# Attention kernel: V product in plain f32, mask inside the row maximum, first rope on VectorE

## The reference, cut to what matters

```python
q = apply_rotary(x @ Wq_h, cos, sin)        # rope: t * cos + rotate_half(t) * sin
k = apply_rotary(x @ Wk_g, cos, sin)
scores = (q @ k.T) * 128 ** -0.5             # positions after the query are hidden
out += (softmax(scores) @ (x @ Wv_g)) @ (Wo_h * head_scale[h])
```

## Time and profile before

| | |
|---|---|
| median of 3 runs | 1413.64 us (1412.12 to 1413.68) |
| the profiled execution's own time | 1417.51 us |
| its span, first to last instruction | 1415.7 us |
| granted TensorE clock, mean | 0.97 of full speed |
| busy: PE / PE weight loads | 1265.8 us (89%) / 1118.0 us (79%) |
| busy: DVE / ACT / POOL | 823.7 (58%) / 734.8 (52%) / 687.0 us (49%) |

### The profile page before, as it was taken

How to read it: one execution, slowest core, us unless ns; L and a number is a source line. 1 busy time by engine, 2 the same in 40 slices (tenths; PEclk the granted TensorE clock), 3 DMA queues, 4 the chain that set the end, 5 groups by cost and what they waited for, 6 DMA issues and landing times. The chain is left out here.

```text
span 1415.7 us, 23253 instructions
## 1 busy us (share of the span) xinstructions
PE 1265.8 (89%) x8288; PEld 1118.0 (79%) x8288; DVE 823.7 (58%) x1642; ACT 734.8 (52%) x1407; POOL 687.0 (49%) x454
## 2 busy tenths in 40 slices
PE   4698999999999998999899999988798989799995
PEld 3587888888888787888788888876687878687984
DVE  0265666665665576566566666665454655855556
ACT  1355555565565555666566655543456445255342
POOL 4766457467465464756845744302345325225250
PEclk9699999999999999999999999998899999999997
DMA  4113112112111020111111200000000000001000
GB/s 122 45 46 108 27 28 60 27 28 52 36 27 38 23 53 23 39 27 46 42 27 27 61 23 20 24 2 14 8 8 16 8 9 16 1 16 45 9 8 30
DMA packets 41472, 44.92 MB, mean 32 GB/s; under 512 B 12680, under 2 KB 35720, under 8 KB 41104
## 3 DMA queue, kind: packets, MB, share of 16 engines
q1 hardware_dynamic: 39888, 41.34, 11.5%
q10 hardware_dynamic: 1472, 2.11, 0.5%
HBM read 20.36 MB, written 2.10 MB: 16 GB/s over the span
## 5 line engine op out<-in xcount | busy, mean ns | idle before, releaser
L626 ACT ACTIVATE exp_parts<-turned 128x512 fp32r<-128x512 f32 (+1 forms) x320 | 177.6, 555 | 358.9 <-PE turned L481 358.1
L728 DVE TENSOR_TENSOR exp_parts<-turned,exp_parts 128x512 fp32r<-128x512 f32 (+1 forms) x320 | 202.9, 634 | 209.0 <-ACT exp_parts L626 208.8
L464 PE MATMUL ring<-kT,qT 128*128 128x512 f32 (+3 forms) x1152 | 270.7, 365 | 41.9 <-ACT exps L617 30.5
L500 PE MATMUL mix<-exp_parts,v_sb 128*128 128x256 f32 (+1 forms) x1920 | 293.8, 289 | 0.0
L500 PEld LDWEIGHTS mix<-exp_parts,v_sb 128*128 128x128 f32 x1920 | 252.8, 191 | 3.6
L464 PEld LDWEIGHTS ring<-kT,qT 128*128 128x128 f32 x1152 | 189.4, 192 | 74.5 <-ACT exps L617 42.9
L722 DVE TENSOR_REDUCE neg_max<-ring 128x1 f32<-128x128 f32 (+7 forms) x256 | 189.3, 749 | 45.6 <-PE ring L467 45.5
L617 ACT ACTIVATE exps<-ring,neg_max 128x128 f32<-128x128 f32 (+7 forms) x256 | 188.4, 739 | 21.4 <-DVE neg_max L722 16.7
L823 POOL TENSOR_TENSOR cos_part<-taken,cos_sb 128x1024 f32<-128x1024 f32 x40 | 95.5, 2388 | 202.9 <-ACT taken L596 202.9
L481 PE MATMUL turned<-ident,exps 128*128 128x128 f32 x1152 | 181.2, 275 | 0.0
L826 POOL TENSOR_TENSOR rotated<-rotated,sin_sb 128x1024 f32<-128x1024 f32 x40 | 95.5, 2389 | 79.7 <-DMA rotated<-taken 79.7
(11 more groups left out here) (179 smaller groups left out, 1887.5 us busy)
## 6 DMA issues: line engine op xcount, KB each, us to landing
rotated<-taken SPq DMA_DIRECT2D x80, 256.0 KB, 3.7
raw_q<-in_L_attn_Wq_dram SPq DMA_DIRECT2D x32, 128.0 KB, 3.5
raw_o<-in_L_attn_Wo_dram SPq DMA_DIRECT2D x32, 128.0 KB, 3.6
exps_and_mu<-in_L_ffn_mu_dram SPq DMA_DIRECT2D x1, 2048.0 KB, 9.4
ffn_w_sb<-in_L_ffn_W_dram SPq DMA_DIRECT2D x16, 128.0 KB, 2.5
ffn_w_sb<-in_L_ffn_W_dram SPq DMA_DIRECT2D x8, 256.0 KB
out_dram<-y_sb SPq DMA_DIRECT2D x4, 512.0 KB, 3.4
y_sb<-in_L_attn_x_dram SPq DMA_DIRECT2D x1, 1024.0 KB, 10.1
```

Source lines behind the costliest of these rows:

```text
L464: last = nc.tensor.matmul(ring_cols(item, lo, hi - lo), qT[:, H % QUERIES, a, i * P:(i + 1) * P], kT[:, G % 2, m, lo:hi], start=k == 0, st ...
L500: last = nc.tensor.matmul(out, v_sb[:, G % 2, a, j * P:(j + 1) * P], parts[:, m, cols], start=j == 0 and k == 0, stop=alone and k == 2)
L626: nc.scalar.activation(exp_parts[:, n % HELD, 0, 0:width], turned[:, n % 2, 0:width], ACT.Copy).then_inc(done[kind], 1)
L728: nc.vector.tensor_tensor(exp_parts[:, n % HELD, 1, 0:width], turned[:, n % 2, 0:width], exp_parts[:, n % HELD, 0, 0:width].bitcast(F32), ...
```

## The change

1. **V product.** V is kept as one plain f32 tensor and each half tile is one plain f32 matmul in place of three. `exps_hi` and `exps_lo` become one copy per tile, on ACT for even tiles (`copy_a`) and on DVE for odd ones (`copy_b`). `v_hi` and `v_lo` become one ACT copy (`v_copy`).
2. **Mask.** The mask matmul goes. `max` becomes a `tensor_tensor_reduce`: it adds a row of the constant `hidden` (SBUF, zeros with the mask at the end), negates, writes the block back to PSUM, and reduces with min; `exp` then takes `scale=-1`. It is two instructions on DVE: the pass and a read of its accumulator.
3. **First rope.** K and Q of head 0 are projected in halves of 512 columns (`first`), and DVE does the rope straight from PSUM (`near`, `far` in two ops of 64 partitions that read across, `join`, `part_lo`), with ACT rounding (`part_hi`). POOL and the swap DMAs have no part in it. Scores 0 and 1 of head 0 are planned before the second half.
4. **Loads.** `ident` and x of sequence 0 go first, then weights of K and Q, cos and sin, then V; x of sequence 1 is loaded after the start, behind the first rope swap on SP's queue. PE waits for `ident` alone. Weights of query 2 are made ahead of head 0's loop.

```diff
-    for who, n in (("v", 0), ("k", 0), ("q", 0), ("q", 1)):
-        weights(who, n)
+    weights("k", 0)
+    weights("q", 0)
+    plan.append(("load_tables",))
+    weights("v", 0)
+    weights("q", 1)
...
+    def pieces(half):
+        for who in ("k", "q"):
+            plan.extend([(kind, who, half) for kind in ("near", "far", "join", "part_hi")])
+        plan.extend([("part_lo", who, half) for who in ("k", "q")])
+
+    plan.extend([("first", "k", 0), ("first", "q", 0), ("project", "v", 0), ("first", "k", 1), ("first", "q", 1)])
+    pieces(0)
+    plan.append(("take", "v", 0))
+    for i in range(2):
+        plan.extend([("scores", 0, i), ("max", 0, i), ("exp", 0, i)])
+    pieces(1)
+    plan.append(("turn_v", 0))
     rope("q", 1)
+    plan.extend([("v_copy", 0)])
+    weights("q", 2)
+    out_weights(0)
     settle()
-    out_weights(0)
-    for i in range(6):
+    for i in range(2, 6):
         top(0, i)
         settle()
-    split_rope("q", 1)
-    weights("q", 2)
...
+        if H == 0 and n == 2 and sequences > 1:
+            plan.append(("load_x", 1))
-        plan.extend([("turn_exps", H, w, p), ("exps_hi", H, w, p), ("exps_lo", H, w, p)])
+        plan.extend([("turn_exps", H, w, p), ("copy_a" if step % 2 == 0 else "copy_b", H, w, p)])
...
-        v_sb = sb("v_sb", [P, 2, 2, N], F32R)
+        v_sb = sb("v_sb", [P, 2, N])
-        exp_parts = sb("exp_parts", [P, HELD, 2, BANK], F32R)
+        exps_turned = sb("exps_turned", [P, HELD, BANK])
...
-            pe.wait_ge(consts_ready, 2)
+            pe.wait_ge(ident_loaded, 16)
...
-                                                    kT[:, G % 2, m, lo:hi], start=k == 0, stop=k == 2 and not diagonal)
-                        if diagonal:
-                            last = nc.tensor.matmul(ring_cols(item, width - P, P), ident_b[:, :], hidden_b[:, :],
-                                                    start=False, stop=True)
+                                                    kT[:, G % 2, m, lo:hi], start=k == 0, stop=k == 2)
...
-                        for k, (a, m) in enumerate(PARTS):
-                            last = nc.tensor.matmul(out, v_sb[:, G % 2, a, j * P:(j + 1) * P], parts[:, m, cols],
-                                                    start=j == 0 and k == 0, stop=alone and k == 2)
+                        last = nc.tensor.matmul(out, v_sb[:, G % 2, j * P:(j + 1) * P], exps_turned[:, n % HELD, cols],
+                                                start=j == 0, stop=alone)
...
-                                         bias=neg_max[:, H % 2, i:i + 1], accum_out=row_sum[:, H % 2, i:i + 1]
+                                         bias=neg_max[:, H % 2, i:i + 1], scale=-1.0, accum_out=row_sum[:, H % 2, i:i + 1]
...
-                    nc.vector.tensor_reduce(neg_max[:, H % 2, i:i + 1], ring_cols(("scores", H, i), 0, (i + 1) * P),
-                                            AX_X, ALU.max, negate=True).then_inc(done[kind], 1)
+                    nc.vector.tensor_tensor_reduce(tile, tile, hidden[:, N - width:N], -1.0, 3.0e38, ALU.add, ALU.min,
+                                                   neg_max[:, H % 2, i:i + 1]).then_inc(done[kind], 1)
...
+                    nc.vector.tensor_copy(exps_turned[:, n % HELD, 0:width], turned[:, n % 2, 0:width]).then_inc(done[kind], 1)
```

More of the change, by code:

```diff
@@ L147, in plan_attention @@
             top(H, 6 + n // 2)
+        if H == 0 and n == 1:
+            split_rope("q", 1)
         if n == 1 and ahead:
@@ L387, in free_ring @@
                         pe.wait_ge(done["xT_lo"], count("xT_lo", *which))
+                    if kind == "first":
+                        pe.wait_ge(done["far"], count("far", *which))
                     if kind == "project":
@@ L428, in _ @@
                     last.then_inc(done[kind], 1)
+                if kind == "first":
+                    who, half = which
+                    w = wk_sb if who == "k" else wq_sb[:, 0]
+                    pe.wait_ge(done["weights_lo"], count("weights_lo", who, 0))
+                    pe.wait_ge(done["xT_lo"], count("xT_lo", 0, KT - 1))
+                    free_ring(item)
+                    passes = [(c, a, m) for c in range(KT) for a, m in PARTS]
+                    for k, (c, a, m) in enumerate(passes):
+                        last = nc.tensor.matmul(ring_cols(item, 0, BANK), w[:, a, c, :], xT[0][:, m, c, half * BANK:(half + 1) * BANK],
+                                                start=k == 0, stop=k == len(passes) - 1)
+                    last.then_inc(done[kind], 1)
                 if kind == "project":
@@ L601, in _ @@
                     wait_stage(act, "weigh", SHARE * (G - 1) - 1, 3, 3)
-                    nc.scalar.activation(v_sb[:, G % 2, 0, :], ring_cols(("turn_v", G), 0, N), ACT.Copy).then_inc(done[kind], 1)
+                    nc.scalar.activation(v_sb[:, G % 2, :], ring_cols(("turn_v", G), 0, N), ACT.Copy).then_inc(done[kind], 1)
+                if kind == "part_hi":
+                    who, half = which
+                    dst = kT if who == "k" else qT
+                    cols = slice(half * BANK, (half + 1) * BANK)
+                    act.wait_ge(done["join"], count("join", *which))
+                    nc.scalar.activation(dst[:, 0, 0, cols], cos_part[:, "kq".index(who), cols], ACT.Copy).then_inc(done[kind], 1)
                 if kind == "rope_hi":
@@ L625, in _ @@
                         act.wait_ge(done["weigh"], n - HELD + 1)
-                    nc.scalar.activation(exp_parts[:, n % HELD, 0, 0:width], turned[:, n % 2, 0:width], ACT.Copy).then_inc(done[kind], 1)
+                    nc.scalar.activation(exps_turned[:, n % HELD, 0:width], turned[:, n % 2, 0:width], ACT.Copy).then_inc(done[kind], 1)
                 if kind == "mixed_hi":
@@ L712, in _ @@
                                             xT[b][:, 0, c, :].bitcast(F32), ALU.subtract).then_inc(done[kind], 1)
[L713 to L717 removed]
+                if kind in ("near", "far", "join", "part_lo"):
+                    who, half = which
+                    cols = slice(half * BANK, (half + 1) * BANK)
+                    part = cos_part[:, "kq".index(who), cols]
+                if kind == "near":
+                    dve.wait_ge(done["first"], count("first", *which))
+                    dve.wait_ge(done["load_tables"], 2 * 16)
+                    nc.vector.tensor_tensor(part, ring_cols(("first", who, half), 0, BANK), cos_sb[:, cols], ALU.mult).then_inc(done[kind], 1)
+                if kind == "far":
+                    if count(kind, *which) > 1:
+                        dve.wait_ge(done["join"], count(kind, *which) - 1)
+                    far = ring_cols(("first", who, half), 0, BANK)
+                    nc.vector.tensor_tensor(rotated[0:64, cols], far[64:128], sin_sb[64:128, cols], ALU.mult)
+                    nc.vector.tensor_tensor(rotated[64:128, cols], far[0:64], sin_sb[0:64, cols], ALU.mult).then_inc(done[kind], 1)
+                if kind == "join":
+                    dve.wait_ge(done["near"], count("near", *which))
+                    dve.wait_ge(done["far"], count("far", *which))
+                    nc.vector.tensor_tensor(part, part, rotated[:, cols], ALU.subtract).then_inc(done[kind], 1)
+                if kind == "part_lo":
+                    dst = kT if who == "k" else qT
+                    dve.wait_ge(done["part_hi"], count("part_hi", *which))
+                    nc.vector.tensor_tensor(dst[:, 0, 1, cols], part, dst[:, 0, 0, cols].bitcast(F32), ALU.subtract).then_inc(done[kind], 1)
                 if kind == "max":
```

91 lines of the change are left out of this document (46 added, 45 removed).

## The result

The changed kernel takes 1360.11 us (median of 4 runs, 1356.79 to 1360.80) against 1412.88 for the kernel before on the same chip: a ratio of 0.9624, 95% interval 0.9605 to 0.9643. It is 53 us faster, where 108 were forecast; 1360 lies outside the range. The profiled execution took 1356.79 us, its span 1355.0, at a granted clock of 0.977.

A forecast was written before the change was run, and what follows sets the result against it. PE's own work was taken to bound most of a head, with ACT and DVE chains close under it. 90 us from 32 heads plus 22 at the start gave 112 off 1417.5; adjusted forecast 1305 us, range 1270 to 1345.

The forecast's parts named there:

- A plain f32 matmul of 256 columns takes (1043.63 - 1040.18) / 16 = 0.216 us: Price of the new V product's matmul on PE, read from the earlier trace: 0.216 us for 256 columns.
- Wide half tile: 3 x 0.119 - 0.216 = 0.141 us saved: V product on PE: one plain f32 matmul replacing three f32r saves 0.141 us, 16 times a head: 2.26 us.
- Plain f32 costs four passes here: Rival, chance 0.02: V product on PE grows 0.9 us a head, masks give 0.98 back, only the start gains: about 1390.
- The masks: Dropping the mask matmuls takes 0.12 us each off PE, 8 a head: 0.98 us.
- The fused maximum: DVE's new maximum runs at the plain reduction's full rate, plus an accumulator read of 0.15 us, 1.2 us a head.
- The waits at tiles 5 to 7: PE's waits in the head loop: tiles 5 and 6 stay, tile 7's falls to some 0.6, averaging 0.35 us less a head.
- The waits at tiles 0 and 4: PE's waits for exponentials in the head loop: tile 0's grows by 0.8 us, tile 4 gets a new one of about 0.65.
- The start: Before the head loop: new loads and first rope bring scores 0 at 25, the first turn at 38.5, 18 us earlier.
- PE's wait of 4.1 us for query 2's weights: At 63.32 us in the earlier trace: this wait goes, since the weights now stand ahead of query 1's rope on POOL.
- rope chain on POOL: Rival, chance 0.12: in the head loop POOL's rope comes late and ACT stands at `rope_hi`: 1343 us.
- Sum: Whole kernel: 90 us from the heads and 22 from the start, 112 us in all; forecast 1305.

The follow-up runs named there:

- v_two: The changed kernel with V split in hi and lo, exponentials rounded to f32r without their lo part, two f32r matmuls a half tile: 1322.1 us.
- exp_first_no_mask: exp_first with the mask change undone (bf16 mask matmul and plain reduction back): 1351.9 us.
- copies_act: The changed kernel with the copies of all tiles on ACT instead of alternating with DVE: 1385.6 us.
- no_v: The changed kernel with the V product change undone (three f32r matmuls, hi and lo copies from ACT and DVE): 1388.2 us.
- no_v_both_last: exp_first_no_v with the lo copy planned behind the tile's maximum on DVE; the hi copy stays behind the exponential on ACT: 1329.4 us.
- exp_first: The changed kernel with each tile's copy planned behind the deferred items, such as the exponential on ACT: 1333.3 us.
- before_exp_first: The kernel before the change with its two copies planned behind the deferred items, nothing else changed: 1409.1 us.
- exp_first_no_v: no_v with both copies, hi and lo, planned behind the deferred items: 1407.5 us.

## Why the prediction was wrong

- **The step that failed: "A plain f32 matmul of 256 columns takes (1043.63 - 1040.18) / 16 = 0.216 us",** and with it "Wide half tile: 3 x 0.119 - 0.216 = 0.141 us saved". The gathers of the earlier trace rows were read as 16 matmuls in 3.45 us. The row counts records, and their code has 8 calls (a loop over TILES, which is 8). One call takes 0.43 us. With that, part 1 costs PE 30 us where 94 were to be gained (2.26 + 0.68 us a head). v_two, which has 104 of the forecast's 125 us, takes 1322 us, inside the range: this price carries some 38 of the 55 us between 1305 and 1360. The earlier trace rows and the code at line 1207, read together, would have told it before.
- The rival **"Plain f32 costs four passes here"**, at 0.02, had this price right to the hundredth: 0.9 us a head, given back by the masks. What the Trainium skill says of true f32 (FP8 and Floating Point Precision, TensorE Precision Notes) agrees with the trace once calls are counted: 0.43 us for 256 columns, against the 427 ns that the prediction had estimated from the page and set aside. Its time, 1390, was wrong for another reason: it took the waits as fixed, and they fell by 43 us.
- **The masks**, -0.98 us a head of PE: alone they gave 9 us of their 31, since waits took the rest. With few waits left (exp_first_no_mask) they gave 19.
- **The fused maximum** at the reduction's rate with a read of 0.15: 1.22 and 0.14 us. Right.
- **The waits at tiles 5 to 7.** At tile 6 (scores 3) the wait was to stay, and did: 1.4 us in six of 24 heads. Tile 7's was to shrink to some 0.6 in half of the heads. Before, it stood in ten heads of the loop and not in half of them (the prediction had read one head), and in the change it is gone in all but two, 12 and 16. Tile 5's was to stay too, "DVE is rid of one 0.63 us pass ahead of the maximums, PE arrives 0.7 earlier": it fell from 1.13 to 0.28. Missed was that tile 5's copy moves to DVE as tile 7's does, so that block 0's and 1's exponentials no longer stand behind it: in copies_act the wait is 1.24 again and in v_two, where PE does arrive earlier, 0.34.
- **The waits at tiles 0 and 4.** At tile 0 the wait was to grow by 0.8 and at tile 4 by 0.65. Both hung on a faster PE. In the change tile 0's fell, from 0.44 to 0.11 on average. In v_two, with the faster PE, it grew from 0.26 to 0.81 us in three heads of four (the fourth kept its 0.97), tile 4's by about 0.4 before scores 0 or 1, and that before the output at tile 9 from 0.60 to 1.28 in one head of four. That is a growth of about 0.6 us a head at tiles 9 and 0 and 0.4 at tile 4. So these two places were right and their sizes too large. That the total of v_two still comes near the forecast's share is in part luck: tile 5's fall was not forecast, and neither was 0.3 us more before the V product at tile 3.
- **The start**, forecast 18 us up to the first turn, gave 13.5 between the two traces and about 10 once the slow clock of before is left out. Scores 0 came at 25.93 for "25"; the last pass of the second half ended at 34.5 for "33". Then the sum went from 33 to 38.5 by four score blocks alone; V's transposes (1.6 us) and query 1's projection (4.5 us, at a granted clock of 0.60) stand ahead of them. Without those 6.1 us the turn would be at 36.7 at best (an estimate). Whether another place for them gains was not tried. PE's wait of 4.1 us for query 2's weights went, as forecast; it lies in the loop.
- The **rope chain on POOL** hardly showed: ACT waited for it 4 times, 6.1 us in all.
- **Sum.** Between the profiled executions 112 us were forecast and 60.7 measured. In the loop 94 (90, and the 4.1 for the weights) came to 43; up to the first turn 18 came to 13.5; behind the loop 3.9 went that nobody forecast. That leaves 51 us; the profiled execution after lies 3.3 under its median, which with rounding makes the 55 between 1305 and 1360.

## What to carry to other kernels

Before a duration is taken from a grouped row, divide the row's count by the calls in the code: here one call was two records, and the whole sign of a term hung on it. Where every engine walks one list in order, put what frees a bank ahead of a copy that is due later, and let no engine's next maximum stand behind something that waits for the other engine: with no instruction added or removed that was worth 27 us in one version and 59 in another (no_v to no_v_both_last), while moving the copies only in part cost 19 and 8. One order is not good for every version: try it again once copies are merged or split.

The fastest versions are exp_first, 1333.3 us, and no_v_both_last, 1329.4, with ratios 0.9409 to 0.9454 and 0.9386 to 0.9429: the runs can't tell them apart. In the second the V product is as before, in three f32r matmuls, so part 1 isn't needed for it. On the kernel before, the new order was tried only in the form that keeps lo ahead of the maximum (before_exp_first, 1409.1); what no_v_both_last's order would give there is not shown.

## What was not expected of the hardware

- A plain f32 matmul shows as two records of 0.216 us each at 256 columns (two of 0.109 at 128), while a plain f32 transpose by the identity, 128 columns, is one record of 0.109. The product therefore costs 1.2 times three f32r matmuls at 256 columns and 0.8 times at 128.
- An f32r matmul of 128 columns saves little over one of 256: in no_v_both_last a tile of a wide and a narrow half takes 0.64 us (414.89 to 415.53 in the timeline of PE), so three narrow ones take 0.64 - 0.36 = 0.28, 0.094 each, against 0.119.
- DVE's pass that adds, negates, writes back to PSUM and reduces costs what the plain reduction did (1.224 against 1.215 us at 1024 columns), plus 0.14 us for its result.
- PE's waits may cost twice. exp_first_no_v had half the clock in 38 us of its loop, no_v in 7, and the two stretches looked at begin while PE waits. That the waits bring the clock down is suggested by this and not shown.
